# First loads in other pieces, constants later, one query turn moved, a shorter tile-wise part in the last down chunk

## The reference

```python
Q = x @ WQ.T + bQ
K = (x @ WK.T + bK)    # 512 columns, tiled to 2048
V = (x @ WV.T + bV)    # 512 columns, tiled to 2048
scores = Q K^T, masked causally
attn = softmax(scores) / sqrt(128)
x = layernorm(x + (attn V) @ proj)
g = (x @ gate_w.T) * gate_s;  u = (x @ up_w.T) * up_s
x = layernorm(x + ((silu(g) * u) @ down_w.T) * down_s)
```

## Time and profile before

| | |
|---|---|
| median of 3 runs | 1338.86 us |
| the profiled execution's own time | 1339.91 us |
| its span on the slowest core, core 1 | 1338.3 us |
| TensorE matmul busy | 1288.2 us, 96% |
| VectorE / ScalarE / GpSimd busy | 334.1 / 169.2 / 78.8 us |
| mean granted TensorE clock, core 1 | 0.992 of full |

### The profile page before, as it was taken

How to read it: one execution, slowest core, us unless ns; L and a number is a source line. 1 busy time by engine, 2 the same in 40 slices (tenths; PEclk the granted TensorE clock), 3 DMA queues, 4 the chain that set the end, 5 groups by cost and what they waited for, 6 DMA issues and landing times.

```text
span 1338.3 us, 14897 instructions; the slowest of 8 cores (1331.0 to 1338.3 us)
## 1 busy us (share of the span) xinstructions
PE 1288.2 (96%) x6120; PEld 585.2 (44%) x6120; DVE 334.1 (25%) x528; ACT 169.2 (13%) x251; POOL 78.8 (6%) x149
## 2 busy tenths in 40 slices
PE   5899998998989999999999999999999999999997
PEld 1344443444444444444444444444444444444443
DVE  0023344445777211111101111101110031030445
ACT  0110001133446211101111101111100000000000
POOL 4100010000000000000100000000000000000000
PEclk9899999999999999999999999999999999999999
DMA  9989999237446264344784434343404446474643
GB/s 136 144 201 230 229 255 266 99 122 165 151 150 196 59 119 75 71 91 91 123 151 88 79 67 91 63 89 69 75 20 94 79 79 142 79 143 73 114 143 158
DMA packets 35331, 162.93 MB, mean 122 GB/s; under 512 B 4160, under 2 KB 5056, under 8 KB 22208
## 3 DMA queue, kind: packets, MB, share of 16 engines
q0 software_dynamic: 20880, 92.28, 41.0%
q1 hardware_dynamic: 14384, 69.69, 15.0%
HBM read 237.46 MB, written 16.78 MB: 190 GB/s over the span
## 4 chain that ended last, share of the span: by engine, by line
PE 88%; DMA 7%; DVE 2%; issue 1%; ACT 1%; POOL 1%; DVEq 0%; ACTq 0%; POOLq 0%; SPq 0%
PE pb L643 45%; PE pb L801 22%; PE pb L302 7%; PE pb L297 6%; PE pb L468 2%; DMA xch<-xT 2%; PE pb L526 2%; DMA stg<-prd 2%; DMA stg<-wqd 1%; PE pb L568 1%; DMA dT<-dnd 1%; PE pb L364 1%; DVE y L572 1%; ACT upp L491 0%; PE pb L505 0%
## 5 line engine op out<-in xcount | busy, mean ns | idle before, releaser
L643 PE MATMUL pb<-x1T,gu 128*128 128x512 bf16 x2816 | 610.1, 379 | 0.0
L643 PEld LDWEIGHTS pb<-x1T,gu 128*128 128x128 bf16 x2816 | 275.6, 98 | 331.8 <-issue 1.3
L801 PE MATMUL pb<-dT,hT 128*128 128x512 bf16 x1408 | 306.1, 380 | 3.2 <-DMA dT<-dnd 2.8
L801 PEld LDWEIGHTS pb<-dT,hT 128*128 128x128 bf16 x1408 | 138.1, 98 | 171.0 <-issue 6.3
L661 DVE SCALAR_TENSOR_TENSOR hT<-pb,usc,sil 128x512 bf16<-128x512 f32 x88 | 66.1, 751 | 516.0 <-PE pb L643 516.0
L297 PE MATMUL pb<-xch,wk 128*128 128x512 bf16 x512 | 120.7, 391 | 18.3 <-DMA xch<-xT 17.0
L655 ACT ACTIVATE sil<-pb,gsc 128x512 f32<-128x512 f32 x88 | 60.5, 687 | 513.0 <-PE pb L643 512.9
L302 PE MATMUL pb<-wv,xch 128*128 128x512 bf16 x512 | 117.6, 386 | 4.1 <-DMA wv<-wvd 4.1
L297 PEld LDWEIGHTS pb<-xch,wk 128*128 128x128 bf16 x512 | 50.6, 100 | 83.4 <-issue 28.3
L302 PEld LDWEIGHTS pb<-wv,xch 128*128 128x128 bf16 x512 | 50.3, 99 | 67.6 <-issue 10.1
L822 DVE SCALAR_TENSOR_TENSOR y<-pb,dsb 128x512 f32<-128x512 f32 x32 | 22.0, 691 | 222.4 <-PE pb L801 222.1
(11 more groups left out here) (75 smaller groups left out, 403.5 us busy)
## 6 DMA issues: line engine op xcount, KB each, us to landing
gu<-gud POOLq DMA_DIRECT2D x46, 1024.0 KB, 8.7
dT<-dnd POOLq DMA_DIRECT2D x44, 512.0 KB, 5.2
stg<-wqd SPq DMA_DIRECT2D x16, 1024.0 KB, 18.0
stg<-prd SPq DMA_DIRECT2D x16, 1024.0 KB, 8.7
xch<-xT POOLq DMA_DIRECT2D x28, 512.0 KB, 15.7
y<-xq SPq DMA_DIRECT2D x8, 1024.0 KB, 6.7
x1fd<-y SPq DMA_DIRECT2D x8, 1024.0 KB, 4.4
x1r<-x1fd SPq DMA_DIRECT2D x4, 2048.0 KB, 16.9
```

Source lines behind the costliest of these rows:

```text
L643: tm = P.pe(lambda e, ct=ct: e.matmul(bank[bk][:], gu[s][:, w, ct, :], x1T[tch][:, ct, :], start=(ct == 0), stop=(ct == CT - 1)), [tg, bf[ ...
L801: return P.pe(lambda e: e.matmul(bank[tt][:], hT[tt // 4][:, it, (tt % 4) * 128:(tt % 4 + 1) * 128], dT[s % 8][:, it % 4, :], start=(it == ...
```

## The change

Four edits. The pieces of the first loads become 1, 1, 2, 4, 4, 2, 2 contraction tiles (they were 1, 1, and seven of 2), and chunk 1's load is gated on a piece of wk (was: of x). Of SyncE's constants only the V bias stays early; `bq16`, `idb`, `msk`, `gsc` and `usc` are issued behind `bqr`, and the reduction of `bq16` moves in VectorE's order from the start to the end of chunk 1. The turn of query tile 4 moves from behind K group 1 of chunk 6 to behind V group 1. In the last down chunk `cut` is 16.

```diff
-    cuts0 = [0, 1, 2, 4, 6, 8, 10, 12, 14, 16]
+    cuts0 = [0, 1, 2, 4, 8, 12, 14, 16]
...
-    load_x(1, [t_x[0][12]])
+    load_x(1, [t_wk[12]])
...
-    const("bq16", bq16[:], bqd, [t_x[0][4]])
-    for nm, dst, src in (("idb", idb[:], idbd), ("msk", msk[:], mskd), ("gsc", gsc[:], gsd),
-                         ("usc", usc[:], usd), ("bvb", bvb[:], bvr.broadcast_to([128, DQ]))):
+    const("bvb", bvb[:], bvr.broadcast_to([128, DQ]), [t_x[0][4]])
+    const("bqr", stg[0][:], bqr.unsqueeze(0).broadcast_to([128, 4, DQ]), [t_x[1][15]])
+    for nm, dst, src in (("bq16", bq16[:], bqd), ("idb", idb[:], idbd), ("msk", msk[:], mskd),
+                         ("gsc", gsc[:], gsd), ("usc", usc[:], usd)):
         const(nm, dst, src)
-    const("bqr", stg[0][:], bqr.unsqueeze(0).broadcast_to([128, 4, DQ]), [t_x[1][15]])
-
-    t_bqc = P.ve(lambda e: e.tensor_reduce(bqc[:], bq16[:], axis=AX.X, op=OP.add), [t_c["bq16"]])
+    t_bqc = None
...
-                if j == 6 and dq == 1:
-                    q_turn(4, 7)
         if j == 6:
             folds_pj(2)
         for sv in range(4):
             v_group(j, sv, 4 + sv)
+            if j == 6 and sv == 1:
+                q_turn(4, 7)
...
         if j == 1:
             t = P.ve(lambda e: e.tensor_add(stg[0][:, 0:2, :], stg[0][:, 0:2, :], stg[0][:, 2:4, :]),
                      [t_c["bqr"]])
+
+            t_bqc = P.ve(lambda e: e.tensor_reduce(bqc[:], bq16[:], axis=AX.X, op=OP.add),
+                         [t_c["bq16"]])
...
-        cut = 40 if ch < 3 else 12
+        cut = 40 if ch < 3 else 16
```

## The result

The changed kernel takes 1328.5 us in the median of three runs (1327.74 to 1330.11) against 1338.86 us for the one before. A fourth run, of 1370.62 us, had a low TensorE clock on one die and is left out, as are five of the experiments' 55 (one of e2, one of e3, three of e8) for the same reason. The ratio to the kernel before is 0.992, with a 95% interval of 0.9906 to 0.9934: 0.8% faster, or about 10.5 us. The forecast was 1331.5 us in a range of 1326.5 to 1335. It has the right side and lies inside, but 3 us too high, and one of its terms was wrong.

The account below looks back on a forecast made before the run. TensorE was taken as the bound, with a matmul in flight for 96% of the span. On core 1, -5.3 (turn) - 4.5 (down chunk) + 2.5 (head) = -7.3 us, so the median 1338.86 becomes 1331.5 us, range 1326.5 to 1335.

Parts of the forecast that it names:

- The turn: Query tile 4's turn: TensorE's 3.6 us wait for qn and 1.7 us of half clock go, gaining 5.3 us.
- The rival of the exchanged wait: At the turn, V group 0 waits for bank 4 instead, giving back all 5.3 us: 1336.8 us; chance 0.05.
- The last down chunk: TensorE's 2.8 us wait for a slab of down weights and 1.7 us of half clock go, gaining 4.5 us.
- The clock: Half clock behind TensorE's waits at the turn and the slab, 1.7 us each on core 1, goes with them.
- The constants at their new place: Five small DMAs ahead of the first WQ loads on SyncE fit in some 4 us free, costing nothing.
- The head: First loads and chunk 0's K and V: coarse pieces move its end from 56.0 to 58.5 us, losing 2.5.
- My sign of being wrong: Among the signs of a wrong prediction: the head ends outside 53.5 to 61.5 us.
- the landing of wv of tiles 8 to 11: In the head, this piece lands at 43.6 us: 44.9 less 1.3 for the moved constants.
- the lower bound that I had set, 40.3: In the head, the earliest landing of wv of tiles 8 to 11, for a head's end of 53.5 us.
- The gate of chunk 1's load: Chunk 1's load, gated one landing earlier, hides under K and V of chunk 0: counted as nothing.
- The rival "early head": The head comes out 2.5 us early, total -12.3 us: 1326.5 us; chance 0.25.
- The rival of "six DMAs fewer": Six fewer DMAs land the head's loads 7.5 us earlier, at 36.1, head's end 49.4: 1322.4 us; chance 0.03.

Follow-up runs that it names:

- e2: Kernel before with only cut = 16 (was 12) in the last down chunk: 1335.2 us, ratio 0.9962.
- e3: Kernel before with only the first loads in pieces of 1, 1, 2, 4, 4, 2, 2 tiles: 1340.7 us, ratio 1.0004.
- e8: Changed kernel with one more tiny ScalarE activation ahead of everything, so the table loads early: 1328.2 us, ratio 0.9904.
- e1: Kernel before with only the turn of query tile 4 moved: 1334.4 us, ratio 0.9954.
- e9: The changed kernel run once more, nothing altered, as base for later runs: 1328.0 us, ratio 0.9915 to the kernel before.
- e6: Changed kernel with the first loads in the pieces of before (1, 1, seven of 2): 1330.0 us, ratio 0.9925.
- e4: Kernel before with only the five constants moved behind bqr, and the reduction of bq16 with them: 1338.5 us, ratio 0.9986.
- e10: Changed kernel with the early ScalarE activation and cut = 20 in the last down chunk: 1328.1 us, ratio 0.9912.
- e11: As e10, with chunk 1's load gated on x of tiles 12 and 13 as before the change: 1325.6 us, ratio 0.9895.

## Why the prediction came out as it did

**The turn: right.** Waits of 3.4 us in the mean and the clock behind them went; nothing took their place. The bank that was to be late next is wanted at 230.30 and free at 226.93, which leaves 3.4 us where I had 3.5. VectorE's timeline on core 2:

```profile
224.31 1.23 DVE L243 TENSOR_TENSOR stg<-stg 128x1024 f32<-128x1024 f32 x1 [4.22 <-DMA stg<-prd]
225.64 0.69 DVE L246 TENSOR_TENSOR pjs<-stg 128x512 bf16<-128x512 f32 x1
226.25 0.68 DVE L369 TENSOR_TENSOR qn<-pb,bqb 128x512 bf16<-128x512 f32 x1
```

The value for core 1, 5.3 us, agrees with e1's 5.2. In the mean over the cores the prediction's terms make 3.4 + 7/8 x 1.7 = 4.9, since seven of eight had the clock's loss. The rival of the exchanged wait is refuted.

**The last down chunk: right.** The 4.5 us were for core 1. For the mean of the cores the same terms make 2.6 + 6/8 x 1.7 = 3.9 (mean wait 2.6, the clock's loss on six), and e2 measured 3.6.

**The clock: right, and a third of the gain.** Behind 56 us and ahead of the last stores a core spent 8.1 us at half clock in the mean before, and 1.7 after (2.1 in e9). Half of the difference, about 3.1 us, is time won; 6.0 us are the two waits, 0.4 the head. That is 9.5 of the 10.0 us measured. What is left near 385 us, 3.4 us at half clock on four cores, was there before on five; its cause is open.

**The constants at their new place: right.** No wait came of them, and no idle time of TensorE in chunk 1.

**The sum: inside the range, and the head's term makes the miss.** With the 0.4 us that the heads gained in the mean, in place of 2.5 lost, the same sum gives 1328.7 us, and 1328.5 was measured. That it comes so near has some luck in it, since two terms are core 1's and one is a mean. For core 1 alone the terms make 5.3 + 4.5 + 3.5 = 13.3 us, and its span fell by 14.1; in the mean of the cores they make 4.9 + 3.9 + 0.4 = 9.2, and 10.0 were measured. No one core stays the slowest: it is core 2 in the profiled execution, cores 5 and 1 in the other two.

**The head: wrong in sign.** I wrote that it "loses 2.5 us", on core 1. Core 1 ended its head at 56.0 before and at 52.5 after; the slowest head was 56.2 before and 55.4 after; over the profiled executions with either head (three and five) the means are 54.2 and 53.8, a gain of 0.4. My sign of being wrong, a head's end outside 53.5 to 61.5, is met on core 1. The step that failed is the landing of wv of tiles 8 to 11, "44.9 - 1.3 = 43.6". It came at 36.7 to 39.7, on core 1 at 37.3. I had taken it as a law that the same bytes land at the same time, however they are cut. The pairs that differ in the cuts show that they do not: with the late constants they land at 42.6 in e6 and at 38.4 in the changed kernel, which has the same gate, and with the early ones at 43.4 before and 37.3 in e3. In e3 the constants also come later, but that cannot carry it: e4 has the five out of the way altogether and lands at 41.9. So the lower bound that I had set, 40.3, was too high as well. It rested on a misreading besides: wk, x and wv of tiles 10 and 11 did not land 2 to 4 us apart on core 1, but at 39.2, 43.6 and 44.9. Two things are in the earlier landing. First, the bytes themselves come somewhat faster. The software queue's packets, MB and share of the engines' time between 18 and 27 us on core 1, kernel before:

```profile
q0 software_dynamic: 791, 1.44, 105.1%
q1 hardware_dynamic: 138, 0.02, 2.3%
```

and e3_pieces:

```profile
q0 software_dynamic: 415, 1.50, 103.9%
```

Half the packets move 4% more in the same time, a part of it because SyncE's queue (q1) takes no share there; of the data packets alone, in the mean of all cores those of 2048 bytes took 214 ns and those of 4096 took 401 there, 6% less per byte. Second, and larger: counted over the DMA records of all cores, twelve tiles' worth of bytes had been moved at 36.9 us before, but the piece that completed them landed 6.5 us later; in e3 it is 34.3 us, and 3.0 later. In e6, with small pieces again, it is 37.2 and 5.4. A piece comes in sixteen shares, each with an update of the semaphore of its own in the trace, and counts as landed at the last. For the piece with wv of tile 11 the updates run from 31.0 to 43.4 us before (means of the cores) and from 31.7 to 37.3 in e3; in e6 they run from 32.6 to 42.6, in the changed kernel from 32.5 to 38.4. The first share comes at about the same time, and with small pieces the others are spread over 10 to 12 us instead of 6. The records do not name the engine of a share and do not show why they drift apart. That stays open.

What ate the gain of an early landing were two things that I had counted as nothing or not at all. The gate of chunk 1's load, of which I wrote "I count nothing", costs about 2 us: with `t_wk[12]` chunk 1's load is issued at 39 to 43 us, and the last pieces of chunk 0 land at 50.7 us, against 48.2 with the old gate (e10 and e11). The kernels e4 and e6, which differ in the head by this gate alone, say the same, 52.9 against 54.9 (they ran on different chips). And with wv of 8 to 11 early, the last wait is that for the last piece of wv, with 12 matmuls behind it on the cores that wait there, as core 2 does. So in the head the constants gave 1.2 us (e4, against 54.2), the gate took 2.0 (e4 to e6), and the pieces gave 1.2 (e6 to 53.8). The three make 0.4, and the means of the two heads differ by 0.4. The heads of all the combinations that ran, in us (mean of three kernels in the first field, of five in the last, else one profiled execution, on different chips):

| constants and gate | small pieces | large pieces |
|---|---|---|
| early constants, gate of before | 54.2 | 55.2 (e3) |
| late constants, gate of before | 52.9 (e4) | 52.1 (e11) |
| late constants, early gate | 54.9 (e6) | 53.8 |

The gate costs 1.6 us with large pieces and 2.0 with small ones. But the pieces cost 1.0 us with the early constants and give 0.8 to 1.2 with the late ones, and the late constants give 1.2 us with small pieces and 3.0 with large ones. e3's trace has one sign of why: there the last of the constants lands at 47.1 us, among the last pieces of chunk 0, where it was 42.5 before. No run changes this by itself, so it is not shown.

The rival "early head" had the sign and 1326.5; the measured 1328.5 lies between it and the forecast, 2.0 us from the rival and 3.0 from the forecast. Its reason was another, though: it had the small DMAs slow the landings, and it is the pieces that moved them. The rival of "six DMAs fewer" had a head at 49.4, and is refuted: the landing at tile 8 came nearly as early as it said (38.4 against 36.1), but all bytes still have to land, at 50.4 against 51.4 us. The fixed cost per DMA that the Trainium skill gives ("DMA: Bandwidth & Descriptors", on the GpSimd path) would, by the prediction's estimate, have taken 12 us from the last landing if it were paid once for each DMA. This case does not bear that out: 0.9 us went, and 1.7 from e4 to e11, which have the same gate and the same constants.

## What to carry to other kernels

A short wait of TensorE costs its own length and then the slow stretch behind it; here waits of 3.4 and 2.6 us were worth 5.2 and 3.6 us in the mean of spans (e1, e2), so look for the waits that stand alone and move only the instruction that waits, past work that needs nothing of it. When loads bound a stretch, do not only add up bytes to tell when a piece lands: the same bytes landed 4 to 6 us apart here. Measure it with the pieces cut the new way, and then look at the last landing, not only at the one that was late before. The transfer that is let in next competes with the last pieces of this one, so its gate has an optimum: one landing too early cost 2 us here, four too late 2 to 5 us of waiting.

## What the runs showed that I had not expected

- Larger pieces land sooner than their bytes say: 37.3 us against 43.4 for the same twelve tiles (e3), 38.4 against 42.6 with the late constants (changed kernel, e6). The sixteen shares of a piece spread over 6 us and not over 10 to 12.
- Opening the gate for 2 MB more one landing earlier, while the last pieces are under way, moves the last landing from 48.2 to 50.7 us, although GpSimd issues it behind all of them (e10 and e11).
- The first activation's table load of 1.28 us stands on TensorE's path when the first copies out of PSUM end a stage: 1.4 us of waiting in four parts, 0.3 when the table is loaded in the first microseconds (e8).
- The last store takes 2.7 us on one core and 4.4 on another in the same execution, and that is part of which core is the slowest (changed kernel, cores 7 and 2).
